# When VectorE and TensorE load node-block numbers in the second layer's edge stage of a graph kernel

## The reference, cut to what matters

```python
q, k, v = (qkv[:, 0], qkv[:, 1], qkv[:, 2])
score = jnp.einsum('ehd,ehd->eh', q[dst], k[src]) * SCALE
mx = jax.ops.segment_max(score, dst, num_segments=n)
ex = jnp.exp(score - mx[dst])
denom = jax.ops.segment_sum(ex, dst, num_segments=n)
attn = ex / denom[dst]
msg = attn[:, :, None] * v[src]
h_new = jax.ops.segment_sum(msg, dst, num_segments=n)
```

## Time and profile before

| | |
|---|---|
| median of 3 runs | 2358.1 us (2356.45 to 2360.24) |
| profiled execution, span from first to last instruction | 2476.2 us |
| profiled execution outside that span | not in the records |
| second layer's edge stage in it, about | 1425 to 2165 us |
| share busy over the span: TensorE, VectorE, ScalarE, GpSimd | 77%, 66%, 43%, 46% |

### The profile page before, as it was taken

The page is one execution under the profiler, slowest core; times in us unless marked ns, Lnnn a source line. Parts: engine busy times, 40 slices in busy tenths (PEclk is TensorE's granted clock), DMA queues, the critical chain, the costliest instruction groups (busy, mean ns, idle before and its releaser), DMA issues. The chain is left out here.

```text
span 2476.2 us, 44345 instructions
## 1 busy us (share of the span) xinstructions
PE 1900.7 (77%) x10786; PEld 1621.3 (65%) x10787; DVE 1635.6 (66%) x3035; ACT 1065.9 (43%) x2312; POOL 1127.1 (46%) x1154
## 2 busy tenths in 40 slices
PE   4589899899998989549838477777777777651798
PEld 3478788788887878439827356555655556431698
DVE  4367677677776745425448277778778777687465
ACT  2567677576676635214301344334344343010343
POOL 0455555555554502444434566666667666030200
PEclk8799999999999989569959789999999998785799
DMA  3333233233332212133325555555555555010100
GB/s 98 119 92 99 85 95 97 83 96 92 89 98 84 83 43 83 41 127 121 96 82 191 172 142 153 158 162 153 154 152 166 150 160 153 17 54 2 37 21 32
DMA packets 124320, 255.92 MB, mean 103 GB/s; under 512 B 23428, under 2 KB 68885, under 8 KB 124182
## 3 DMA queue, kind: packets, MB, share of 16 engines
q0 software_dynamic: 61792, 186.60, 26.2%
q1 hardware_dynamic: 61974, 66.65, 8.9%
q10 hardware_dynamic: 416, 1.18, 0.1%
HBM read 221.93 MB, written 34.24 MB: 103 GB/s over the span
## 5 line engine op out<-in xcount | busy, mean ns | idle before, releaser
L1874 POOL DMA_INDIRECT a_rows<-kv_table,a_idx x440 | 474.2, 1078 | 291.1 <-issue 150.6
L317 POOL DMA_INDIRECT e_rows<-h_table,e_idx x440 | 430.3, 978 | 348.9 <-ACT e_idx L324 228.9
L1949 PE MATMUL a_q<-q,a_spread 128*128 x880 | 260.5, 447 | 106.2 <-ACT a_spread L1925 54.9
L1949 PEld LDWEIGHTS a_q<-q,a_spread 128*128 128x128 f32 x880 | 182.8, 218 | 150.3 <-issue 124.4
L695 DVE TENSOR_TENSOR e_msg<-e_w,e_rows 128x1024 f32<-128x1024 f32 x110 | 134.8, 1225 | 197.0 <-PE e_w L614 163.5
L1958 PE MATMUL a_agg<-a_rows,x 128*128 128x264 f32 x880 | 239.7, 420 | 23.4 <-DVE a_rows L2015 15.1
L610 PE MATMUL e_w<-w2h,e_hidl 128*128 128x256 f32 x880 | 251.7, 308 | 0.4 <-DVE e_msg L695 0.4
L582 PE MATMUL e_agg<-e_msg,e_hot 128*128 128x256 f32 x880 | 240.3, 396 | 0.0
L611 PE MATMUL e_w<-w2l,e_hidh 128*128 128x256 f32 x880 | 231.0, 284 | 0.0
L1958 PEld LDWEIGHTS a_agg<-a_rows,x 128*128 128x128 f32 x880 | 180.6, 210 | 71.6 <-issue 21.4
L630 ACT COPY sums<-e_agg x220 | 81.9, 372 | 264.9 <-PE e_agg L582 185.2
(11 more groups left out here) (419 smaller groups left out, 4605.9 us busy)
## 6 DMA issues: line engine op xcount, KB each, us to landing
e_ea<-in_eaT SPq DMA_DIRECT2D x220, 64.0 KB
m_rows<-expert_rows SPq DMA_DIRECT2D x32, 272.0 KB
e_rows<-h_table,e_idx POOLq DMA_INDIRECT x440
a_rows<-kv_table,a_idx POOLq DMA_INDIRECT x440
q_ab<-expert_out SPq DMA_DIRECT2D x50, 128.0 KB, 3.4
kv_table<-q_kv SPq DMA_DIRECT2D x25, 256.0 KB, 2.0
u_stage<-in_m_w SPq DMA_DIRECT2D x16, 256.0 KB
x<-in_x SPq DMA_DIRECT2D x1, 3200.0 KB, 13.4
```

What stands on the lines that cost most here:

```text
L317: c.nc.gpsimd.indirect_dma_start(out=rows[:, g.slot8, j, :], out_offset=None, in_=table, in_offset=bass.IndirectOffsetOnAxis(ap=idx[:, g.s ...
L1874: nc.gpsimd.indirect_dma_start(out=rows[:, g.slot * IG + j, 0:2 * D], out_offset=None, in_=c.kv_dram, in_offset=bass.IndirectOffsetOnAxis( ...
L1949: last = mm(qp[g.pair][:, j * D:(j + 1) * D], spread[:, g.pair, j, :], window(c.q, wins[j // CT]), start=True, stop=True)
```

## The change

Loads move. A small class keeps a loaded value under the step that will use it; a step that finds none loads as before. VectorE loads the number for the next step's L2009 after L2028 and the blocks of place 0 or place 1 that follow it, just ahead of the reduction L2049. In place 1 it there also loads the number for the next step's L2021. TensorE loads the number for the next step's L1949 after this step's L1949. The first step of each loop turn finds nothing kept and loads for itself; what the last step of a turn loads ahead is not used.

```diff
+        self.step = self.n if isinstance(self.n, int) else ("loop", q)
+        self.then = self.n + 1 if isinstance(self.n, int) else ("loop", q + 1)
...
+class Ahead:
+    def __init__(self, load):
+        self.load, self.kept = load, {}
+    def take(self, step, name, n):
+        value = self.kept.pop((step, name), None)
+        return self.load(n) if value is None else value
+    def fetch(self, step, name, n):
+        self.kept[(step, name)] = self.load(n)
...
             def _(pe):
+                ahead = Ahead(lambda n: item_windows(pe, c, n))
...
-                        wins = item_windows(pe, c, g.n)
+                        wins = ahead.take(i.step, "q", g.n)
                         need(pe, None, (s_sp, g.n + 1), (s_pr, g.n - 1), own=True)
                         for j in range(IG):
                             last = mm(qp[g.pair][:, j * D:(j + 1) * D], spread[:, g.pair, j, :], window(c.q, wins[j // CT]), start=True, stop=True)
                         last.then_inc(s_q, 1)
+                    if real(at(2)):
+                        ahead.fetch(i.then, "q", at(2).n)
...
+                ahead = Ahead(lambda n: item_windows(dve, c, n))
...
-                        wins = item_windows(dve, c, a.n)
+                        wins = ahead.take(i.step, "sums", a.n)
...
-                        w, _ = item_windows(dve, c, ch * (CH // IG))
+                        w, _ = ahead.take(i.step, "crossing", ch * (CH // IG))
...
                         v.tensor_scalar(fall[:, :], c.carried[:, 0, 0:1], peak[0:H, 0:1], 0.0, ALU.subtract, ALU.min).then_inc(s_fl, 1)
+                    if real(at(-LAG)):
+                        ahead.fetch(i.then, "sums", at(-LAG).n)
+                    if i.place == 1 and closed(ch):
+                        ahead.fetch(i.then, "crossing", ch * (CH // IG))
                     if real(i):
                         need(dve, s_dg, (s_pr, i.n + 1))
                         v.tensor_reduce(sc[:, i.cslot, i.place * IG:(i.place + 1) * IG, :].rearrange("p t h -> p (t h)"),
```

## The result

| | before | changed |
|---|---|---|
| median, 4 runs each | 2359.17 us (2356.45 to 2361.56) | 2387.23 us (2385.89 to 2393.14) |
| ratio, 95% interval | | 1.0127 (1.0111 to 1.0143) |
| span of the profiled execution | 2476.2, a second one 2359.3 | 2384.2 |
| edge stage, first to last L2009 (changed: L2030) | 703.3 (second one) | 732.6 |

The change makes the kernel 28 us slower; 16 were forecast.

A forecast was written before the change was run, and what follows sets the result against it. VectorE and its sequencer pace the end of place 0 to place 3, elsewhere VectorE or TensorE. +0.84 us x 28 = +23.5, less 4 at place 3, less 4 for tails: +16, 2374 us, range 2347 to 2398.

The forecast's parts named there:

- rival A: Place 1: the two new loads lie bare on VectorE; +1 to +24 us, 2359 to 2382; chance 0.59.
- The four terms on VectorE: Per chunk: place 0 load +0.65, start of place 1 -0.70, place 1 loads +1.28, start of place 2 -0.39 us.
- Removing the crossing's load from place 2: Place 2, VectorE's second load: it ran behind the 1.22 us of L2015, so removing it saves 0.
- the new load on TensorE: TensorE, between queries and sums: hidden because the sequencer is well ahead of its engine, cost 0.
- +20 - 4: Place 0: waits for tails hide 12 us of loads as in the profile; a third of that taken off +20, giving +16.
- Starts of place 3 and place 0: -4 us: VectorE: 0.33 us of idle "issue" given back in each of eleven starts of place 3, -4 us in all.
- the chunk grows by 1.28 - 0.65 = 0.63 us: Start of place 3, where TensorE's sums set it: 0.63 us instead of 0.89; if in all 28, 7 us less.
- rival D: TensorE idles longer ahead of late queries, its clock stays lower: 32 us on top of 16, 2406; chance 0.10.
- D's sign: In the changed profile, a granted clock under 0.9 over the stage points to TensorE staying at its lower clock.
- The slack that the prediction held against D: TensorE's sums of place 2 have slack to place 3 at full clock; no size given.
- Rival B: Every chunk waits for tails, always hiding place 0's load: no change, +1 us, 2359; chance 0.18.
- Rival C: VectorE's sequencer queues the reduction while a load is under way, so only savings stay: -35 us, 2323; chance 0.13.

The follow-up runs named there:

- the second profile: The kernel before, unchanged, profiled once more: span 2359.3 us, edge stage 703.3 us.
- e7_filled: The changed kernel with useless transposes on TensorE in place 1, in its waits for the exponentials and diag: 2353.9 us against 2357.7 for the kernel before, ratio 0.9985.

## Why the prediction was right in its mechanism and wrong in its size

The direction and rival A's mechanism held. The reduction of place 1 moved from 0.12 to 1.42 us after the fall (1.4 forecast), that of place 0 to 0.85 after the ends (0.8), the starts of places 1 and 2 lost their idle time, and the queries followed the correction after 0.52 us (within 0.4). The four terms on VectorE were right one by one: forecast times 28 and measured over 27 chunks, +18.2 and +18.0, -19.6 and -18.9, +35.8 and +33.2, -10.9 and -11.5. Together that is +23.5 against +20.8. Removing the crossing's load from place 2 and the new load on TensorE cost and gave nothing, as said.

Two terms were mis-sized. The step that failed above all is the second: the price of place 3 and of TensorE's path to it, worked out at full clock.

*"+20 - 4": a third of the hidden loads of place 0.* The waits for tails come once, 1.9 us, in the second profile, so hardly anything is hidden and the 4 us were not there to subtract. The sign that the rows gave, a late release in an execution 118 us too long, was read rightly and then discounted only in part.

*"Starts of place 3 and place 0: -4 us", and "the chunk grows by 1.28 - 0.65 = 0.63 us" where TensorE binds.* The starts of places 3 and 0 cost +7.0 - 0.7 = +6.3 us, a miss of 10. TensorE's path did get its load out of the way (1.00 to 0.52 us) and diag came 1.3 us later, but the queries between stayed longer at the lower clock: 74.0 us over 26 chunks before, 87.6 after, or 0.5 us a chunk. So TensorE's path grew by about 1.3 - 0.5 + 0.5 = 1.3 us and VectorE's by 1.3 - 0.4 = 0.9, and the difference is waited for at place 3: 0.4 x 27 = 11 us by this account, of which 7 were measured. The changed kernel's own chunks show what the wait hangs on: in the five whose queries take 1.99 us the start of place 3 takes 1.14 us, with no wait, in the 16 at 3.78 us it takes 2.2 to 2.8, and the other four lie between. This is rival D's wait, a part of its price, on top of A rather than in its stead, and D's sign, a clock under 0.9, came too (0.89). The slack that the prediction held against D was slack at full clock. `e7_filled` shows that the wait goes with the clock. That idle time ahead of the queries brings the lower clock is shown as far as filling it removes it. D's reason for it, more idle time for a late diag, is not needed: the kernel with the loads behind the product has as slow queries without it. Why the queries slowed from 74.0 to 87.6 us stays open.

Rival B fell with the second profile. Rival C fell too: no reduction passed a load, and a third load in the way held it back by another 0.62 us. The rule of the Trainium skill in "Advanced Engine Details and Errata", section "Sequencer Loop", on instructions queued while a control instruction executes, did not help here: with a semaphore instruction between load and reduction, the idle "issue" ahead of the reduction is 1.23 us with two loads and 1.85 with three.

## What to carry to other kernels

In this kernel a register load hides behind the long instruction issued just before it (the product, 1.22 us), if nothing between the two makes the sequencer wait; after a chain of short dependent instructions it is bare and costs 0.6 to 0.7 us at its place. Setting the load for the sums right behind the product, and the crossing's back in its own step, turned +28 us into -23. When a bare stretch goes from one engine, look at what the engine that now binds did just before: here filling TensorE's idle time, and with it the clock, was worth 6 us in the kernel before, where VectorE's load stood ahead of the sums of place 3 too, 33 us in the changed kernel, and 29 us with the loads behind the product.

## What had not been expected of the hardware

Useless transposes on TensorE, 12 a chunk, made the kernel with the well-placed loads 1.2% faster (2334.5 to 2305.4 us): the eight query instructions after the idle time went from up to 3.78 us to 1.99, with the granted clock at 0.97 of full speed over the stage instead of 0.89. And one profiled execution can differ from the runs in the very waits that an argument rests on: 33.1 us for tails in one, 1.9 in the next.
